# A two-layer transformer block on one core: where the last layer's int8 weights are made, and output projection and feed-forward as one loop

## The reference, cut to what matters

```python
# x: (8, 100, 512), ctx: (8, 361, 128)
x = x + L0_xattn(layernorm(x), ctx)      # 16 heads of 32, causal, softmax
x = x + L0_ffn(layernorm(x))             # 8 experts, top 2 of each token
x = x + L1_xattn(layernorm(x), ctx)      # 16 heads of 128, latent keys with rope, out = ctx_lat @ Wo.T
x = x + L1_ffn(layernorm(x))

def _quant_dequant(v, axis):             # of L1_ffn; 127 steps, one scale per row
    scale = jnp.maximum(jnp.max(jnp.abs(v), axis=axis, keepdims=True) / 127.0, 1e-8)
    return jnp.clip(jnp.round(v / scale), -127.0, 127.0) * scale

def L1_ffn(x, w_gate_up, w_down):        # (2816, 512), (512, 1408)
    xq, w1q = quant(x, -1), quant(w_gate_up, -1)
    gate, up = split(xq @ w1q.T)
    hq = quant(silu(gate) * up, -1)
    return hq @ quant(w_down, -1).T
```

## Time and profile before

| | |
|---|---|
| median of three runs | 957.24 us |
| profiled execution | 955.41 us, its span 953.7 us |
| TensorE busy | 785.2 us, 82% of the span |
| VectorE, ScalarE, GpSimd busy | 542.5, 423.2, 248.6 us |
| granted TensorE clock, mean | 0.902 |
| DMA, mean | 93 GB/s over the span, 88.25 MB |
| chain that ended last | TensorE 46%, waits that show no releaser 21%, VectorE 13%, GpSimd 8% |

### The profile page before, as it was taken

One profiled execution on the slowest core, in us unless ns is written; L12 is line 12 of the kernel. 1 busy time (PEld: TensorE's weight loads), 2 busy tenths in 40 slices (PEclk: granted clock), 3 DMA queues, 4 the chain that ended last, 5 costly groups with the idle time before them and its releaser, 6 DMA issues.

```text
span 953.7 us, 14893 instructions
## 1 busy us (share of the span) xinstructions
PE 785.2 (82%) x4828; PEld 625.0 (66%) x4828; DVE 542.5 (57%) x1143; ACT 423.2 (44%) x813; POOL 248.6 (26%) x300
## 2 busy tenths in 40 slices
PE   0889888782999999966889889898878999767674
PEld 0677776582777777865778777787735777545552
DVE  4544344445666666255763655646635677578872
ACT  3432223221556555202763755746634455444441
POOL 1400000002222120332460741725402221123432
PEclk9977888855999999956999999999999999979987
DMA  8400000093375555771010010000164342200000
GB/s 264 162 1 2 0 0 1 11 387 134 94 262 167 177 163 167 254 198 64 1 43 24 31 42 31 33 31 12 47 257 156 125 134 82 75 1 18 17 18 17
DMA packets 28622, 88.25 MB, mean 93 GB/s; under 512 B 6004, under 2 KB 9276, under 8 KB 26272
## 3 DMA queue, kind: packets, MB, share of 16 engines
q1 hardware_dynamic: 23104, 70.49, 21.4%
q0 software_dynamic: 5472, 17.18, 6.4%
HBM read 72.57 MB, written 15.07 MB: 92 GB/s over the span
## 4 chain that ended last, share of the span: by engine, by line
PE 46%; issue 21%; DVE 13%; POOL 8%; DMA 5%; ACT 4%; ACTq 1%; SPq 0%; POOLq 0%; DVEq 0%
PE PS L146 9%; PE PS L148 9%; PE PS L147 9%; POOL wraw L651 5%; PE PS L1061 3%; PE PS L1432 2%; PE PS L1127 2%; PE PS L1415 2%; DMA raw<-wkv_in 1%; DMA fq_raw<-foldq_in 1%; ACT w_hi L743 1%; PE PS L1112 1%; DVE mx L1567 1%; PE PS L1170 1%; DVE xn L126 1%
## 5 line engine op out<-in xcount | busy, mean ns | idle before, releaser
L651 POOL TENSOR_TENSOR wraw<-wraw,rinv 128x361 f32<-128x361 f32 (+1 forms) x104 | 80.9, 789 | 139.3 <-DVE rinv L1624 139.3
L1466 DVE TENSOR_TENSOR w_lo<-w,w_hi 128x1408 fp32r<-128x1408 f32 x40 | 64.9, 1622 | 35.6 <-ACT w_hi L743 35.6
L834 ACT ACTIVATE wraw<-PS,nmx 128x361 f32<-128x361 f32 (+1 forms) x104 | 58.7, 565 | 38.2 <-DVE nmx L1631 30.4
L1631 DVE TENSOR_REDUCE nmx<-PS 128x1 f32<-128x361 f32 (+1 forms) x104 | 55.0, 530 | 33.8 <-PE PS L148 33.8
L743 ACT CAST w_hi<-w 128x1408 fp32r x40 | 54.7, 1370 | 18.6 <-DVE rows L1559 9.7
L603 POOL DMA_INDIRECT xb<-xn_scratch,rows x20 | 34.8, 1739 | 105.0 <-PE PS L1035 102.0
L146 PE MATMUL PS<-w_hi,xt_hi 128*128 128x352 f32 x160 | 56.8, 355 | 5.2 <-DVE xt_lo L1460 4.9
L1634 DVE TENSOR_TENSOR pt_lo<-PS,pt_hi 128x384 fp32r<-128x384 f32 x96 | 52.2, 546 | 12.0 <-ACT pt_hi L840 11.1
L1226 PE MATMUL PS<-ident,wraw 128*128 128x128 f32 x312 | 52.1, 277 | 6.3 <-POOL wraw L651 3.8
L1061 PE MATMUL PS<-w,ht 128*128 128x512 f32 (+1 forms) x120 | 54.9, 593 | 0.6 <-DVE ht L1478 0.6
L146 PE MATMUL PS<-pf_hi,cx_hi 128*100 128x512 f32 x128 | 51.5, 403 | 3.9 <-DVE pf_lo L1770 3.9
(11 more groups left out here) (262 smaller groups left out, 2198.5 us busy)
## 6 DMA issues: line engine op xcount, KB each, us to landing
w<-w_in SPq DMA_DIRECT2D x20, 768.0 KB, 5.4
w<-w_in SPq DMA_DIRECT2D x8, 1408.0 KB, 10.3
fq_raw<-foldq_in SPq DMA_DIRECT2D x6, 1088.0 KB, 8.3
cx_raw<-ctx_scratch SPq DMA_DIRECT2D x8, 800.0 KB, 5.2
ctx_scratch<-ctxo SPq DMA_DIRECT2D x24, 256.0 KB, 2.0
wraw<-wup_in POOLq DMA_DIRECT2D x22, 256.0 KB
ys_scratch<-yb SPq DMA_DIRECT2D x20, 256.0 KB
wraw<-wdown_in POOLq DMA_DIRECT2D x4, 704.0 KB
```

The source lines that it names most:

```text
L651: pool.tensor_tensor(P1[slot][0:rows, 0:NK], P1[slot][0:rows, 0:NK], rinv[0:rows, jj, t:t + 1].broadcast_to((rows, NK)), ALU.mult).then_in ...
L834: act.activation(P1[t % 8][r, 0:NK], PS[r, t % 4, 0:NK], ACT.Exp, bias=nmx[r, jj, t:t + 1], accum_out=rsum[r, jj, t:t + 1]).then_inc(C["ex ...
L1466: dve.tensor_tensor(WL[which][:, :], w12_of(dve_wlo.e, which), WH[which][:, :].bitcast(F32), ALU.subtract) \
L1631: dve.tensor_reduce(nmx[r, jj, t:t + 1], PS[r, t % 4, 0:NK], AX.X, ALU.max, negate=True).then_inc(C["max"], 1)
```

## The change

The weights' work leaves the projection and moves into the first attention, where each quantity is loaded twice, from two arrays prepared outside the program: plain (output rows on partitions) and turned (input rows on partitions).

- SP loads a set's plain tiles into `wraw`; VectorE takes maxima, scales and inverses only (`dve_scale`, three maxima and two short operations), of set n + 1 in batch n, ahead of the residual add.
- SP stores scales and inverses to DRAM (`share_scales`), waits for them, and loads the inverses back on all 128 partitions.
- GpSimd multiplies the turned tile by the inverses, ScalarE adds the magic number (`act_magnify(n)`, behind exp of n + 1), GpSimd subtracts it and writes bf16; SP stores that to DRAM (`store_set`). The transposes, copies and diagonal matmuls are gone.
- The first two of the fold weights (`foldq`), which used `wraw` from the start, are loaded after the last store, in the routing stage.
- When the second attention ends, SP loads all rounded weights and scales back, 5.6 MB.
- Projection and feed-forward are one loop by batch: `pe_ffn(n)` puts a quarter of the projection of batch n + 3 behind each chunk of gate/up of n + 1. The projection has one bank (6) instead of two; statistics and root of the last layer norm are made batch by batch, so that ScalarE changes between the tables of root and silu in each turn. Loops are written out.

```diff
+            load_plain(0)
+            load_turned(0)
+            load_turned(1)
             sp.wait_ge(A["wlo"], 2)
...
+            share_scales(0)
+            load_plain(1)
+            for n in range(1, B):
+                share_scales(n)
+                load_plain(n + 1)
+                store_set(n - 1)
+                load_turned(n + 1)
+            share_scales(B)
...
+            def share_scales(n):
+                at, k = ups_of(n)
+                down = down_of(n)
+                sp.wait_ge(W["inv"], n + 1)
+                for q in range(2):
+                    sp.dma_start(sc_scratch[q:q + 1, at:at + k * 128].rearrange("o (t p) -> (o p) t", p=128),
+                                 WSC[n % 2][:, 0:k, q + 1], allow_slow_non_contiguous=True).then_inc(W["scst"], 16)
...
+                sp.wait_ge(W["scst"], 16 * SHARED[n + 1])
+                wait(sp, W["mul"], TURNED[n - 1] if n >= 2 else 0)
+                sp.dma_start(INVB[n % 2][:, 0:k * 128], sc_scratch[1:2, at:at + k * 128].broadcast_to((128, k * 128))) \
+                    .then_inc(W[f"lt{n % 2}"], 16)
...
+            for n in range(B + 1):
+                pool.wait_ge(W[f"lt{n % 2}"], 16 * ARRIVED[n + 2])
+                at = 0
+                for buf in parts(n, RAWT[n % 2]):
+                    c, w = buf.shape[1], buf.shape[2]
+                    pool.tensor_tensor(buf, buf, INVB[n % 2][:, None, at:at + w].broadcast_to((128, c, w)), ALU.mult).then_inc(W["mul"], 1)
+                    at += w
+                pool.wait_ge(W["mag"], n + 1)
+                wait(pool, W["st"], 16 * TURNED[n])
+                pool.tensor_scalar(whole(n, STAGE), whole(n, RAWT[n % 2]), MAGIC, None, ALU.subtract).then_inc(W["sub"], 1)
...
+            def act_magnify(n):
+                act.wait_ge(W["mul"], TURNED[n + 1])
+                t = whole(n, RAWT[n % 2])
+                act.activation(t, t, ACT.Identity, bias=mgc[:, 0:1]).then_inc(W["mag"], 1)
...
+            sp.wait_ge(C["pv"], NG * B)
+            sp.dma_start(W1Q[:, :, :], w1_scratch).then_inc(FFNW, 16)
+            sp.dma_start(S1B[:, :], sc_scratch[0:1, 0:2 * FI].broadcast_to((T, 2 * FI))).then_inc(FFNW, 16)
+            sp.dma_start(W2Q[:, :, :], w2_scratch).then_inc(FFNW, 16)
...
-            def pe_ffn(n, j, more=True):
+            def pe_ffn(n, j):
+                more = n + 3 < B
                 for c in range(GC - 1):
-                    pe_gate_up(n + 1, 1 - j, c)
+                    if n + 1 < B:
+                        pe_gate_up(n + 1, 1 - j, c)
+                    if more:
+                        project(n + 3, 1 - j, HEADS[c])
                 pe_ht(n, j)
-                pe_gate_up(n + 1, 1 - j, GC - 1)
                 if more:
+                    project(n + 3, 1 - j, HEADS[GC - 1])
+                if n + 1 < B:
+                    pe_gate_up(n + 1, 1 - j, GC - 1)
+                if n + 2 < B:
                     pe_xq(n + 2, j)
                 pe_down(n, j)
+            for n in range(2):
+                project(n, n, range(NH0))
             pe_xq(0, 0)
-            pe.wait_ge(W["ev"], UT + DT)
+            pe.wait_ge(FFNW, 16 + 64)
             for c in range(GC):
                 pe_gate_up(0, 0, c)
+                project(2, 0, HEADS[c])
+            pe_xq(1, 1)
```

More of the change, by code:

```diff
@@ L465, in _ @@
                 sp.dma_start(xn_scratch[b * T:(b + 1) * T], XN[:, b, :]).then_inc(E["xnst"], 16)
+            store_set(B)
+            sp.wait_ge(W["st"], 16 * TURNED[B + 1])
+            for i in range(2):
+                sp.dma_start(FQR[i], foldq_d[i]).then_inc(C["fq0"], 16)
             def load_block(i):
@@ L722, in _ @@
             pool_h(0, 0)
[L723 to L730 removed]
+            for n in range(B):
+                if n + 1 < B:
+                    pool_h(n + 1, (n + 1) % 2)
+                pool_add(n, n % 2)
         def act_xt(act, i):
@@ L879, in batch @@
                     act_attn0_q(act, queries)
-                if not (isinstance(n, int) and n == B - 1):
+                if n < B - 1:
                     act_attn0_exp(act, n + 1, 1 - j)
+                act_magnify(n)
             act_attn0_q(act, 0)
+            act.wait_ge(A["vones"], 2)
             act_attn0_exp(act, 0, 0)
-            batch(0, 0, 1)
-            with act.Fori(0, B // 2 - 2) as p:
-                batch(2 * p + 1, 1)
-                batch(2 * p + 2, 0, p + 2)
-            for n in range(B - 3, B):
-                batch(n, n % 2)
+            for n in range(B):
+                batch(n, n % 2, n // 2 + 1 if n % 2 == 0 and n + 2 < B else None)
             act_attn0_oh(act, B - 1)
@@ L1278, in batch @@
                     pe_attn0_out(pe, n - 1)
-            batch(0, 0, 1)
-            pe.wait_ge(A["wlo2"], 2)
-            with pe.Fori(0, B // 2 - 2) as p:
-                batch(2 * p + 1, 1)
-                batch(2 * p + 2, 0, p + 2)
-            for n in range(B - 3, B):
-                batch(n, n % 2)
+            for n in range(B):
+                if n == 1:
+                    pe.wait_ge(A["wlo2"], 2)
+                batch(n, n % 2, n // 2 + 1 if n % 2 == 0 and n + 2 < B else None)
             pe_attn0_ot(pe, B - 1)
@@ L1375, in _ @@
+            HEADS = [range(h, h + 4) for h in range(0, NH0, 4)]
             pe.wait_ge(O["pfl"], NH0)
[L1376 to L1387 removed]
@@ L1681, in batch @@
                 dve_attn0_norm(dve, n)
+                dve_scale(n + 1)
                 if not first:
                     dve_attn0_add(dve, n - 1)
-            batch(0, 0, 1)
-            with dve.Fori(0, B // 2 - 2) as p:
-                batch(2 * p + 1, 1)
-                batch(2 * p + 2, 0, p + 2)
-            for n in range(B - 3, B):
-                batch(n, n % 2)
+            for n in range(B):
+                batch(n, n % 2, n // 2 + 1 if n % 2 == 0 and n + 2 < B else None)
             dve_attn0_low(dve, B - 1)
```

422 lines of the change are left out of this document (190 added, 232 removed).

## The result

The changed kernel takes 989.12 us (median of four runs, 984.31 to 989.56) against 956.68 before: ratio 1.034, 95% interval 1.029 to 1.039. I had forecast 929, and 914 to 951 as the range. The profiled execution has a span of 987.1 us.

What follows compares the result with a forecast made beforehand. TensorE was taken to bound the output projection, while in the feed-forward it waits about 3.2 us a batch. Terms: 957.2 - 39.9 (last stage) + 10.5 (first attention) + 1.0 (routing) = 928.8, say 929; range 914 to 951.

Steps and rivals of the forecast that it cites:

- The way L: First attention: time from a set's last scale to the inverses landed on all partitions, taken as 7 us.
- the prediction's own terms: First attention, odd sets 1, 3, 5, 7: delays of L - 4.2, L - 6.4, L - 5.8 and L - 2.4 where positive.
- the first maxima: First attention: the first set's maxima and scales stand ahead of the first softmax, half covered, costing 1.3 of 2.4 us.
- The upper bound: First attention: L at most 14.9 us, from 6.8 for packets, 2.0 for the stores to land and 4.2 for the load.
- From the second set on they are covered: First attention: VectorE's maxima and scales, 2.4 to 3.3 us a set, fit its waits for the out matmuls.
- The third: First attention: store-wait-load of inverses decides every odd batch; slower from L = 14.1, 960 at 14.9; 6 in 100.
- The last stage: Merged projection and feed-forward: TensorE's work fills the waits, gain 39.9 us, 35 to 45 with pauses at half or double.
- a turn: Merged loop: TensorE's projection, gate/up, down and small transposes of one turn take 19.3 us, with no wait booked.
- The pauses ahead of them: Last stage before the merged turns: pauses for context splits and quantising; over 15 us in sum would prove the prediction wrong.
- Rival 2: Merged loop keeps the feed-forward's waits, 5 x 3.2 = 16 us, time 945; 12 in 100.
- The drain at a change of tables: Merged loop: about 1.38 us beside each table load; two switches take 2.8 us on ScalarE, all the slack; not booked.
- Routing and after: Routing: normalisations may meet the last multiply and fold weights load only after the last store; 1 us, 0 to 4.

Runs made afterwards that it cites:

- e10: Changed kernel storing scales and inverses as 128 rows of 36 bytes, inverses and final scales loaded from input rows, every engine's order kept: 926.5 us, ratio 0.970.
- e8: DMAs alone, nothing computed, each group waited for: an odd set's 768 single elements took 17.6 us, 128 rows of 36 bytes 1.4.
- e9: DMAs alone again, varying distance and row size: 128 single elements side by side took 7.0 us, 64 bytes apart 1.4, 12-byte rows end to end 2.0.
- e1: Changed kernel with inverses loaded from rows of an input, without waiting for the stores, which are still made: 976.7 us, ratio 1.022.
- e15: Changed kernel with GpSimd rounding alone, plain tiles issued before the wait for scales, single elements issued on ScalarE's DMA queue: 964.6 us, ratio 1.012.

## Why the prediction was wrong, step by step

- **The way L is the step that failed**: "Elements of 4 bytes are nearest to the small stores, so I take 2.0 to land each, 1 for the packets: L = 7." It was 16.7, 15.4, 24.3 and 23.4. With these, the prediction's own terms give 12.5 + 9.0 + 18.5 + 21.0 = 61.0, and with 1.0 for the first maxima 62 of the 74 that the attention paid: the mechanism was there, its size wrong by 13 us a set. The small stores that I took as nearest have rows of 256 bytes a partition, and size and packets were not what decided. The upper bound failed too: 48 packets an engine at 0.141 us made 14.9, because a bound from the time of packets knows nothing of a wait behind them. e10 is the test: with rows in place of elements, stand-in rows in the loads, and the order as it was, 926.5.
- **"From the second set on they are covered"** failed with it. The maxima were covered, but not the wait for their tiles. The loads stand behind the elements and behind SyncE's wait, and VectorE waited 38.9 us ahead of the residual add. I had asked what the stores' landing holds on ScalarE, and not what is queued behind them on SyncE. Nor had the sum a term for VectorE's small operations beside GpSimd, 12.8 us in nine sets, part of it on the way of the scales.
- **The rivals.** The third named the right place, price and direction: from L = 14.1 the kernel is slower. It got 6 in 100, since it hung on an upper bound that was too low, and its 960 is too little: at 20 us the second hold and the lower clock come on top (TensorE's same matmuls took 17 us longer). I did not separate these two in the 12 us that the terms leave over.
- **The rule of the Trainium skill** (DMA: Bandwidth & Descriptors, Rules for kernel authors) that a non-contiguous last dimension becomes one descriptor per element pointed the right way, and I gave it no weight in the sum. The packets agree (144 for 128 elements), but the runs don't bear out the element as the price: 64 bytes apart the same 128 take 1.4 us, side by side 7.0.
- **The last stage was right in its mechanism**: 45.6 us gained where I had 39.9 with 35 to 45, just above; a turn of 18.9 where I had 19.3; no wait of TensorE within the merged turns, as booked. The pauses ahead of them were shorter than I summed. Rival 2 did not come.
- **The drain at a change of tables**, which by the Trainium skill (ScalarE: Activation LUTs, What ACT_TABLE_LOAD costs) would take 1.38 us beside each load, is not in this trace. ScalarE's timeline in a turn:

```profile
870.79 1.28 ACT L1010 ACT_TABLE_LOAD   x1
872.12 0.20 ACT L1010 ACTIVATE std<-veps 100x1 f32<-100x1 f32 x1
872.34 1.28 ACT L1025 ACT_TABLE_LOAD   x1
873.69 0.50 ACT L1025 ACTIVATE gs<-gs 100x352 f32<-100x352 f32 x1
```

  Root, load and silu stand 0.02 to 0.07 us apart.
- **Routing and after** cost 4.1 us (74.9 to 79.0) where I had 1, 0 to 4. The late fold weights aren't it: TensorE waits 6.5 us for them, and waited 8.2 before. Its waits for GpSimd's `tok_of` (6.7 us against 5.1) and for `xt_lo` (6.4 against 4.9) have the size of the first two steps of 1.6. I ran nothing on it.

## What to carry to other kernels

Before a small DMA goes on a path that others wait for, look at its access pattern: single elements side by side in DRAM cost 7 us or more here (128 of them 7 to 9, 768 of them 8 to 18), and the loads issued behind them land late; turn such columns into rows on TensorE first. When a wait is removed and the time hardly moves, look whether the transfer now waits among the DMAs, and whether a second engine has the same hold. When a change of queue helps, look whether it also changed the order of issue. And keep GpSimd's instructions short where VectorE has small work that is due.

## What the runs showed of the hardware

- 128 elements of 4 bytes to neighbouring addresses take 6.8 to 9.1 us in e8 and e9, 64 bytes apart 1.4, in rows of 12 bytes end to end 2.0; the slow and the fast ones are 144 packets each, and those of the slow ones are over about 1 us after the issue.
- DMAs behind them on SyncE's queue land late (13 us in e1, against 2.9 alone). Beside them on another queue tiles of 256 KB took 11.2 and 15.7 us in e15, against 3.0 ahead of them.
- Additions and products of VectorE on few columns (`TENSOR_SCALAR`, and the subtraction for `wg_lo`) waited for the end of GpSimd's instruction, up to 7.48 us, and got in between pieces of 512 columns. Its maxima didn't wait: three of 512 columns took 1.87 us beside GpSimd's multiply (at 95.78 in the changed kernel) and 1.86 without (at 49.21). The Trainium skill (SBUF — State Buffer, SBUF: two separate sides) calls the shared port pair an exclusive lock for the whole instruction, taken by whichever starts first of GpSimd and some of VectorE's operations; by that rule the loser blocks to the end, and the trace agrees: 205.28 against 205.25.
- GpSimd adds and subtracts in one instruction in 8.40 us for 2432 columns where the subtraction alone took 6.36: rounding there costs 2.0 us and takes no step of ScalarE.
